# Relative attention: four heads side by side in a DRAM line instead of two

## The reference

```python
dist = jnp.clip(idx[None, :] - idx[:, None], -R, R) + R
pe_k = rel_emb_k[dist]
pe_v = rel_emb_v[dist]
...
q = q / jnp.sqrt(jnp.asarray(hd, x.dtype))
score = jnp.einsum('bhqd,bhkd->bhqk', q, k) + jnp.einsum('bhqd,qkd->bhqk', q, pe_k)
attn = jax.nn.softmax(score, axis=-1)
ctx = jnp.einsum('bhqk,bhkd->bhqd', attn, v) + jnp.einsum('bhqk,qkd->bhqd', attn, pe_v)
```

## Time and profile before

| | us |
|---|---|
| median of 3 runs | 1876.62 |
| lowest, highest | 1875.46, 1883.51 |
| the profiled execution's own time | 1877.84 |
| its span | 1876.0 |
| mean granted TensorE clock | 0.932 of full speed |

### The profile page before, as it was taken

The page is one execution under the profiler, slowest core; times in us unless marked ns, Lnnn a source line. Parts: engine busy times, 40 slices in busy tenths (PEclk is TensorE's granted clock), DMA queues, the critical chain, the costliest instruction groups (busy, mean ns, idle before and its releaser), DMA issues. The chain is left out here.

```text
span 1876.0 us, 38522 instructions
## 1 busy us (share of the span) xinstructions
PE 1631.2 (87%) x14742; PEld 1280.3 (68%) x14742; DVE 1210.7 (65%) x3881; ACT 676.7 (36%) x1408; POOL 272.1 (15%) x240
## 2 busy tenths in 40 slices
PE   5789997899997678888888677498899999999998
PEld 4577775666655556677776556386688788878876
DVE  2555565455554735566666439627989889888894
ACT  2333332245556246556665333014223222222210
POOL 1344344200000100000000004301001000100000
PEclk9899998999999878999999877599999999999999
DMA  3100000000010278989898450242000000000000
GB/s 122 46 18 18 17 12 18 12 19 25 30 53 29 92 264 308 317 294 327 313 324 316 138 143 18 80 202 91 1 2 13 13 2 13 13 2 13 2 7 13
DMA packets 96469, 175.32 MB, mean 93 GB/s; under 512 B 16032, under 2 KB 80800, under 8 KB 91552
## 3 DMA queue, kind: packets, MB, share of 16 engines
q1 hardware_dynamic: 96288, 172.85, 26.6%
HBM read 93.01 MB, written 79.69 MB: 92 GB/s over the span
## 5 line engine op out<-in xcount | busy, mean ns | idle before, releaser
L104 PE MATMUL bank<-per_xT,per_down 128*128 128x256 f32 x1024 | 250.1, 389 | 2.3 <-ACT per_xT L2380 1.6
L2683 PE MATMUL bank<-per_up,per_act_w 128*128 128x256 f32 x1024 | 242.4, 382 | 0.0
L2683 PEld LDWEIGHTS bank<-per_up,per_act_w 128*128 128x128 f32 x1024 | 195.1, 191 | 26.8
L104 PEld LDWEIGHTS bank<-per_xT,per_down 128*128 128x128 f32 x1024 | 190.2, 192 | 29.9 <-issue 2.7
L2387 ACT ACTIVATE per_act_w<-bank 128x512 f32<-128x512 f32 x128 | 76.2, 597 | 362.9 <-PE bank L104 328.3
L1488 ACT ACTIVATE rel_probs<-rel_summed,rel_low 128x256 f32<-128x256 f32 x256 | 117.2, 518 | 25.7 <-DVE rel_low L1572 25.7
L1572 DVE CUSTOM_DVE_ANT_0 rel_summed<-bank,rel_bias 128x256 f32<-128x256 f32 x256 | 95.0, 419 | 34.6 <-DMA rel_bias<-rel_qr_rows 17.3
L104 PE MATMUL bank<-ret_x2T,ret_w_in 128*128 128x256 f32 x384 | 96.7, 410 | 16.5 <-DVE ret_x2T L442 16.5
L900 DVE TENSOR_REDUCE xat_mx<-bank 128x2 f32<-128x512 f32 x128 | 79.5, 684 | 32.9 <-PE bank L948 32.9
L104 PEld LDWEIGHTS bank<-ret_x2T,ret_w_in 128*128 128x128 f32 x384 | 77.4, 206 | 30.7 <-DVE ret_x2T L442 11.6
L1707 PE MATMUL bank<-rel_band_k,rel_qT 32*128 32x191 f32 x512 | 63.2, 369 | 31.2 <-DVE rel_low L1572 24.0
(11 more groups left out here) (354 smaller groups left out, 3190.9 us busy)
## 6 DMA issues: line engine op xcount, KB each, us to landing
rel_qr_rows<-rel_qr SPq DMA_DIRECT2D x32, 1024.0 KB, 8.5
rel_p_rows<-rel_probs SPq DMA_DIRECT2D x32, 1024.0 KB, 6.7
rel_bias<-rel_qr_rows SPq DMA_DIRECT2D x64, 384.0 KB, 4.4
rel_by_dist<-rel_p_rows SPq DMA_DIRECT2D x64, 384.0 KB, 4.5
per_down<-in_per_down SPq DMA_DIRECT2D x1, 4096.0 KB, 24.8
per_up<-in_per_up SPq DMA_DIRECT2D x1, 4096.0 KB, 12.6
ret_xin<-in_x SPq DMA_DIRECT2D x8, 256.0 KB, 2.8
xat_cT<-in_contextT SPq DMA_DIRECT2D x8, 256.0 KB, 2.8
```

Source lines behind the costliest of these rows:

```text
L104: last = pe.matmul(dst, wt[:, c], src[:, c, :], start=c == 0, stop=c == DC - 1)
L2683: last = pe.matmul(tiles(bank[7])[:, t, :], act_w[:, n % 2, k, t * P:t * P + P], up[:, k, :], start=k == 0, stop=k == COLS - 1)
```

## The change

In the four tiles the two pairs become one group of four: `qr` goes from [2, 2, ROW, 2] to [2, ROW, 4], `bias`, `probs` and `by_dist` alike. An entry of head r is at [position, r], and neighbouring positions of one head are 16 bytes apart. A DRAM line stays as long, 2048 floats, but holds the positions of four heads side by side; the skewed pitch goes from 2 x PW - 2 with PW = 1024 to PW - 4 with PW = 2048. A load takes one run of 3072 bytes from each line instead of two of 1536. The bytes, the number of instructions and of DMA issues, their order on every engine and the semaphores stay. The rest follows from the layout: the strides of the copies, exponentials, bias sums, far sums and transposes.

```diff
-    PW = 2 * ROW
+    PW = 4 * ROW
...
-    qr = sb("qr", [2, 2, ROW, 2])
-    bias = sb("bias", [2, TT, 2, SEQ, 2])
+    qr = sb("qr", [2, ROW, 4])
+    bias = sb("bias", [2, TT, SEQ, 4])
...
-    probs, pT = sb("probs", [2, 2, WIDE, 2]), sb("pT", [4, 4, TT, SEQ])
-    by_dist, wT = sb("by_dist", [3, TT, 2, NEAR + 1, 2]), sb("wT", [2, 2, 2, SEQ])
+    probs, pT = sb("probs", [2, WIDE, 4]), sb("pT", [4, 4, TT, SEQ])
+    by_dist, wT = sb("by_dist", [3, TT, NEAR + 1, 4]), sb("wT", [2, 2, 2, SEQ])
...
-        row = qr[:, U % 2, r // 2, :, r % 2]
-        return bass.AP(row.tensor, row.offset, [list(row.ap[0]), [2 * (BAND + P), TT], [2, BAND]])
+        row = qr[:, U % 2, :, r]
+        return bass.AP(row.tensor, row.offset, [list(row.ap[0]), [4 * (BAND + P), TT], [4, BAND]])
...
-                    for t, first in ((0, 2 * NEAR), (1, 0)):
-                        skewed = bass.AP(p_rows[U % 2].tensor, first, [[2 * PW + 2, P], [PW, 2], [1, 2 * NEAR]])
-                        sp.dma_start(by_dist[:, U % 3, t, :, 0:NEAR].rearrange("p h k e -> p h (k e)"), skewed)\
+                    for t, first in ((0, 4 * NEAR), (1, 0)):
+                        skewed = bass.AP(p_rows[U % 2].tensor, first, [[PW + 4, P], [1, 4 * NEAR]])
+                        sp.dma_start(by_dist[:, U % 3, t, 0:NEAR].rearrange("p k r -> p (k r)"), skewed)\
...
-                    for t, first in ((0, 2 * (P - 1)), (1, 2 * (2 * P + REACH - 2))):
-                        skewed = bass.AP(qr_rows[U % 2].tensor, first, [[2 * PW - 2, P], [PW, 2], [1, 2 * NEAR]])
-                        sp.dma_start(bias[:, U % 2, t, :, REACH * t:REACH * t + NEAR]
-                                     .rearrange("p h k e -> p h (k e)"), skewed).then_inc(bias_loaded[U % 2], 16)
+                    for t, first in ((0, 4 * (P - 1)), (1, 4 * (2 * P + REACH - 2))):
+                        skewed = bass.AP(qr_rows[U % 2].tensor, first, [[PW - 4, P], [1, 4 * NEAR]])
+                        sp.dma_start(bias[:, U % 2, t, REACH * t:REACH * t + NEAR]
+                                     .rearrange("p k r -> p (k r)"), skewed).then_inc(bias_loaded[U % 2], 16)
...
-                    last = nc.scalar.activation(probs[:, U % 2, r // 2, at:at + SEQ, r % 2], summed[:, r, t], ACT.Exp,
+                    last = nc.scalar.activation(probs[:, U % 2, at:at + SEQ, r], summed[:, r, t], ACT.Exp,
...
-                                                    bias[:, U % 2, t, r // 2, :, r % 2], 1.0, 3.0e38, ALU.add, ALU.min,
+                                                    bias[:, U % 2, t, :, r], 1.0, 3.0e38, ALU.add, ALU.min,
...
-                rows = by_dist[:, U % 3].rearrange("p t h k e -> p t h e k")
-                dve.tensor_reduce(rows[:, 0, :, :, NEAR], rows[:, 0, :, :, 0:REACH + 1], AX.X, ALU.add)
-                dve.tensor_reduce(rows[:, 1, :, :, 0], rows[:, 1, :, :, P:NEAR], AX.X, ALU.add).then_inc(far_ready, 1)
+                rows = by_dist[:, U % 3].rearrange("p t k r -> p t r k")
+                dve.tensor_reduce(rows[:, 0, :, NEAR], rows[:, 0, :, 0:REACH + 1], AX.X, ALU.add)
+                dve.tensor_reduce(rows[:, 1, :, 0], rows[:, 1, :, P:NEAR], AX.X, ALU.add).then_inc(far_ready, 1)
...
                         last = pe.transpose(bank[4 + r % 2][:, (2 * c + t) * P:(2 * c + t) * P + P],
-                                            probs[:, U % 2, r // 2, at:at + P, r % 2], ident[:])
+                                            probs[:, U % 2, at:at + P, r], ident[:])
...
                         last = pe.transpose(bank[6][:, (2 * e + t) * P:(2 * e + t) * P + P],
-                                            by_dist[:, U % 3, t, k, first:first + P, e], ident[:])
+                                            by_dist[:, U % 3, t, first:first + P, 2 * k + e], ident[:])
```

More of the change, by code:

```diff
@@ L1327, in relative_attention_layer @@
     st, mv, ve, rs = sb("st", [2, TT, 6]), sb("mv", [2, TT, 2]), sb("ve", [2, 2]), sb("rs", [2, 2])
-    qr_rows = [nc.dram_tensor(f"rel_qr_rows{k}", (P, 2, PW), F32, kind="Internal").ap() for k in range(2)]
-    p_rows = [nc.dram_tensor(f"rel_p_rows{k}", (P, 2, PW), F32, kind="Internal").ap() for k in range(2)]
+    qr_rows = [nc.dram_tensor(f"rel_qr_rows{k}", (P, PW), F32, kind="Internal").ap() for k in range(2)]
+    p_rows = [nc.dram_tensor(f"rel_p_rows{k}", (P, PW), F32, kind="Internal").ap() for k in range(2)]
     ident_loaded, loaded, wv_loaded, late = sem("ident_loaded"), sem("loaded"), sem("wv_loaded"), sem("late")
@@ L1436, in _ @@
                         sp.wait_ge(dist_loaded[(U - 2) % 3], 32 * ((U - 2) // 3 + 1))
-                    sp.dma_start(p_rows[U % 2], probs[:, U % 2, :, REACH:REACH + ROW]
-                                 .rearrange("p h k e -> p h (k e)")).then_inc(p_saved[U % 2], 16)
+                    sp.dma_start(p_rows[U % 2], probs[:, U % 2, REACH:REACH + ROW]
+                                 .rearrange("p k r -> p (k r)")).then_inc(p_saved[U % 2], 16)
                 if (U := table_of(s)) is not None:
@@ L1444, in _ @@
                         sp.wait_ge(bias_loaded[U % 2], 32 * (U // 2))
-                    sp.dma_start(qr_rows[U % 2], qr[:, U % 2].rearrange("p h k e -> p h (k e)"))\
+                    sp.dma_start(qr_rows[U % 2], qr[:, U % 2].rearrange("p k r -> p (k r)"))\
                         .then_inc(qr_saved[U % 2], 16)
@@ L1556, in _ @@
         def _(dve):
-            dve.memset(qr[:, :, :, BAND:BAND + P], 0.0)
-            dve.memset(qr[:, :, :, 2 * BAND + P:ROW], 0.0)
+            dve.memset(qr[:, :, BAND:BAND + P], 0.0)
+            dve.memset(qr[:, :, 2 * BAND + P:ROW], 0.0)
             dve.memset(v[:, :, :, :, HD:VW], 1.0)
-            dve.memset(bias[:, :, 0, :, NEAR:SEQ], 0.0)
-            dve.memset(bias[:, :, 1, :, 0:REACH], 0.0)
-            dve.memset(probs[:, :, :, SEQ:WIDE - SEQ], 0.0)
+            dve.memset(bias[:, :, 0, NEAR:SEQ], 0.0)
+            dve.memset(bias[:, :, 1, 0:REACH], 0.0)
+            dve.memset(probs[:, :, SEQ:WIDE - SEQ], 0.0)
             dve.drain()
```

## The result

| | us |
|---|---|
| kernel before, median of 4 runs | 1877.69 |
| changed kernel, median of 4 runs | 1959.15 (1956.59 to 1962.78) |
| ratio | 1.0422, 95% interval 1.0398 to 1.0445 |
| profiled execution of the changed kernel: time, span | 1962.78, 1961.0 |

The changed kernel is slower by 81.5 us. The forecast was 1964, so its number and its sign held. One of the two mechanisms behind it did not, as the rows show at once.

The account below looks back on a forecast made before the run. Bound by the chain through VectorE's bias sums and TensorE's table matmuls and transposes: 3.11 to 3.57 us more a step, 100 to 114 over 32, less 19.9 of waits, middle plus 87, giving 1964; range 1868 to 1998.

Parts of the forecast that it names:

- the two mechanisms: Relative-attention step's chain: dearer bias sums, 1.68 to 2.14 us a step, and dearer weight loads, 1.43 us a step.
- What bounds the layer: Relative-attention step: a chain of scores, eight bias sums, the table's second part behind the last sum, then transposes; 8.68 us shortest.
- Long runs bring nothing directly: Skewed DMA loads: half as many runs save at most 0.26 us a step, worth nothing while loads are in time.
- The wait for the loads: Bias sums waiting for their DMA loads: 19.9 us over the layer, all expected to go as steps lengthen.
- Bias sums +0.21, exponentials +0.20, VectorE's table copy +0.31: VectorE and ScalarE instructions at a 16-byte step: added us for each, from 1.86 ns per 16 bytes touched.
- Weight loads +0.119 us, 1.43 us of each step: TensorE transposes at a 16-byte step: each 0.119 us dearer, the 12 after the table adding 1.43 us a step.
- a price per access: Other reading of TensorE's weight loads: 0.93 ns per access, so 16 bytes cost no more than 8; the lower bound.
- Table copies and exponentials hidden: VectorE's copies end at 912.9, before scores at 914.3, exponentials earlier; longer steps cost up to 0.4 us more, left to the range.
- Rival (c): Only VectorE and ScalarE pay, 1.68 to 2.14 us a step less 19.9 us of waits: 1918; chance 0.12.
- Rival (a): The 16-byte step costs the engines nothing and only the loads change: 1873, or 1864 if faster; chance 0.31.
- rival (b): Only TensorE's weight loads pay, 2.13 us a step, less some 14 us of waits: 1931; chance 0.07.
- DMA share under 0.75, packets halved: Signs in the layer: DMA share under 0.75 instead of 0.86, and skewed loads with half as many packets under 2 KB.

Follow-up runs that it names:

- long-runs kernel: Kernel before, with one run of 3072 bytes in place of two of 1536 and the old 8-byte step in SBUF: 1885.43 us, ratio 1.0033.
- the block of probes: Changed kernel plus a block ahead of the first layer repeating single instructions at element steps of 4 to 64 bytes; VectorE read 426 ns at 8, 631 at 16.
- the first two kernels: Half the change each against the kernel before: only qr, bias and qr_rows as fours, 1950.84 us; only probs, by_dist and p_rows as fours, 1899.41 us.

## Why the prediction was right, and where it was not

- **What bounds the layer**: right. Only the steps between the sums changed, and the place is the one named, the table's second part behind the last sum.
- **Long runs bring nothing directly**: right, and shown alone (ratio 1.0033). The wait for the loads, 19.9 us with the 2.6 of unnamed cause, was to go whole; it fell to 7.2, a single wait. In the long-runs kernel it was 19.1 us and the unnamed 2.3, so it went because the steps grew, as the prediction had it.
- **Bias sums +0.21, exponentials +0.20, VectorE's table copy +0.31**: +0.198, +0.218, +0.295. ScalarE's table copy was +0.38 for 0.31. The price taken from three sparse facts, 1.86 ns for each 16 bytes touched, is right for these engines: the block of probes gives 205 ns for 256 elements on VectorE and 231 on ScalarE between 8 and 16 bytes, where it gave 210 and 205. It even gives the step that was not forecast: at 12 bytes it is 1.40 ns an element, which with the fixed part of VectorE's time (426 ns less 256 x 1.04) makes about 517 ns, and 516 was measured. The Trainium skill (Advanced Engine Details and Errata, SBUF Cachelines) states the rule in kind: lines of 16 bytes, and at least two hits on a line for full rate. The probes agree at 8 and 16 bytes (426 and 631 ns on VectorE), except for the weight loads, which are longer at 8 already (208 ns for 140) and no longer at 16.
- **Weight loads +0.119 us, 1.43 us of each step**: wrong. This step failed by choosing between two readings of the same fact. The prediction named the other, a price per access for which 16 bytes are as 8, and set it aside because one formula fitted three engines. Its row for TensorE did not bear the formula: the 0.119 us from one weight load to the next was read as what a step of 8 bytes costs, but the trace of before has eight loads of neighbouring elements too:

```profile
919.34 0.90 PEld L1791 LDWEIGHTS bank<-rel_ident,rel_oU 128*128 128x128 f32 x8
```

That is (0.90 - 0.14) / 7 = 0.109 us from one to the next without any step, so nearly all of the 0.119 is the pace of the transposes themselves. 209 ns before and after, and 1886.08 us with only the transposes at 16 bytes, show that the term is nothing.

- **Table copies and exponentials hidden**: wrong. In the prediction's sum only sums and weight loads stand. Taken back in this order, the sums gave 40 us, the copies 21 and the exponentials 15. They are hidden in the short step shown, where VectorE's copies end at 956.81 and the scores start at 958.39, but in steps with projections, gather or output the next TensorE instruction (lines 97, 104 and 112) waits for ScalarE's table copy, which stands behind the exponentials. The prediction saw this wait, put it at up to 0.4 us and left it to the range: by the step above it is 0.69.
- **Why the number came right**: the terms put in were 1.68 to 2.14 us a step for the sums and 1.43 for the loads, minus the waits; the layer's steps grew by 2.6 on average. In place of the 1.43 that did not exist came what was called hidden, and the time that TensorE runs at its lower clock behind longer waits, which was in no term. The loads' 1.43 us were 46 of the forecast's 87; without them the same sum gives 1918. Two errors of opposite sign met, which is luck; a reader who trusted the sum for its result would have carried the weight-load price to the next kernel.
- **Rival (c)**, only VectorE and ScalarE pay, was the true case by the rows (weight loads at 209, sums at 617), and its price, 1918, was 41 us short for the same two reasons. It had 0.12; of the forecast's own signs the weight loads, 330 ns or 209, told the two apart.
- **Rival (a)**, that the step is free, fell with the first row; **rival (b)** with the first two kernels.
- **DMA share under 0.75, packets halved**: 0.79, 0.62 and 0.66 in three windows of 40 us, and 0.71 from 700 to 1040. Right for the layer.

## What to carry to other kernels

Interleaving several rows so that a DMA run becomes longer is paid by every engine instruction that then walks the tile; with 4-byte elements two abreast are nearly free, four abreast cost VectorE, ScalarE and TensorE's moving operand 0.7 to 1.0 ns an element, and here nothing was gained by runs longer than 1536 bytes. Before a term is hidden behind another engine's work, look at the steps that have extra instructions there, not only at the shortest one: the cover differs from step to step. And where a cost is inferred from one kind of access (a read of an operand), a weight load needs a row of its own, and the pace of several in a row, not the duration of one.

## What the runs showed of the hardware

- The step law for 4-byte elements in SBUF: 426 ns for 256 at 8 bytes, 516 at 12, 631 at 16, 605 at 64 on VectorE; reading and writing alike, ScalarE much the same. It is flat from 16 on, as was expected, and near half of the cost is there at 12, where little was.
- Weight loads of 128 columns: 140 ns at 4 bytes, 208 at 8, and then 194 to 237; in a row of transposes they follow each other after 0.109 us at 4 bytes and 0.120 at 8 and 16.
- Two runs of 1536 bytes or one of 3072, the sums' waits for them were the same (17.3 and 19.1 us).
- TensorE's granted clock was 0.96 over four steps in which it was not busy for 4.8 us, and 0.78 over the same steps when it was not busy for 8.9. The lower level showed behind the waits, where eight transposes took 1.91 us instead of 1.04, and one engine's dearer instructions were paid a second time in TensorE's own work.
